# The order of the tensor engine's three pieces in an attention step: output products moved from behind the projection's part to directly behind the scores

## The chip, the cores and the metric

The kernel runs on one core of a Trainium2 chip. A core has a matrix engine (TensorE: PE in the profile, with PEld for its weight loads), three engines for elementwise work (VectorE: DVE, ScalarE: ACT, GpSimd: POOL), and a queue engine (SyncE: SP) that here only issues transfers. Each of them runs its own list of instructions in order, and they wait for each other through semaphores. The metric is the device time of the program in microseconds (us); before the change its median is 2392.17 us over 3 runs (2389.41 to 2393.09).

## The reference: what is computed

A transformer layer on an input x of 2 batches by 2048 tokens by 1024 channels, with 16 heads of width 64:

```python
x = x + layernorm(attention(layernorm(x)))
x = x + layernorm(ffn(layernorm(x)))
# attention
q, k, v = (x @ w.T + b for w, b in ...)           # heads of 64
scores = q @ k.T / 8, causal mask
out = softmax(scores) @ v;  out @ wo.T + bo
# ffn: 8 experts, a gate picks one per token, low-rank update of rank 8
```

The change concerns attention alone. The ffn follows in a later phase of the program.

## The kernel before, in words

**Pairs, rounds, steps.** The 32 (batch, head) problems are done as 16 pairs of heads (`p` = 0 to 15; pairs 8 to 15 are the second batch). In each pair the 16 query tiles of 128 rows are done two at a time, a long one and a short one, in 8 rounds. A round is cut into 2 or 3 steps of at most 8 key blocks of 128, a pair has 17 steps (`NSTEP`). A step whose `opens` is set starts a round, one whose `closes` is set ends it. In pairs 1 to 14 the closing steps are 1, 3, 5, 8, 10, 12, 14, 16; in pairs 0 and 15 they are 1, 3, 5, 7, 9, 11, 13, 16.

**What one step does on TensorE.** `body` of the tensor block runs three pieces per step `i`:

- `scores(i + 3)`: the score products of the step three further on (`LAG` = 3), for both heads, into two of three tiles `s_ps` (line 529). Every number is carried as a high and a low fp16 part, so each product is three matmuls. It waits until the exponential of an earlier task has freed its tile (`exp_done`).
- `project(...)`: a part of one projection unit of the next pair (lines 598 to 604). A unit is 512 tokens of q, k or v; it takes one step or is split over two (`UNIT_STEPS`). Its result lies in the one bank `u_ps`. The last matmul of a unit signals `unit_done`.
- `times_v(i, h)` for the two heads: transposed probabilities `pt` times v into `o_ps` (lines 552 to 554), 48 matmuls of 65 columns when the step has 8 blocks. It waits for the transposed tile (`pt_done`), and in an opening step also for `part_done` and `short_done`: the sums of the round before must have been read out of `o_ps`, of which there is one set.

**What follows each piece.** After the scores VectorE finds row maxima (`row_max`, lines 732, 737, 742), ScalarE takes exponentials and makes the high half (914, 921), GpSimd makes the low half (1072), and SyncE issues a transposing transfer for each head (419, `transpose_probs`), which waits until earlier output products have released their blocks of `pt` (`pv_done`). After a unit VectorE adds the bias and takes the result out of `u_ps` (`unit_full`, lines 711 for v and 716 for q and k). After a round VectorE reads `o_ps` (`output_read`, lines 760, 762, 766); line 766 signals `short_done`.

**VectorE's order in a step `i`.** `output_read` of the round that closed in step `i - 1` (only if `i` opens a round), `row_min`, `row_max(i + 3)`, `output_sum`, a weight's low half where one is due (698, 700), `unit_full` of the unit that ends in step `i`, and then, in pairs 0 to 6, pieces of the normalization of the second batch (`norm_stats` 661 and 668, `norm_apply` 676, `xn_low` 681; each of 16 tiles has one of each, every second or so step). This order isn't touched by the change.

**Which steps end a unit.** In pairs 1 to 5 and 8 to 13 ("mid"): 0, 1, 2, 4, 5, 7, 8, 10, 11, 13, 14, 16, of which v are 8, 10, 11, 13. In pair 0: 0, 1, 3, 5, 6, 7, 8, 10, 11, 13, 14, 16 (v: 8, 10, 11, 13). In pairs 6 and 7: 0, 1, 2, 4, 5, 6, 7, 9, 11, 12, 14, 16 (v: 1, 4, 9, 14). In pair 14: 1, 3, 5, 7, 9, 11, 13, 15 (k, k, k, q, q, v, v, v). In pair 15: 0, 1, 2, 4 (k, q, q, v), and from step 5 on that pair has no projection at all.

Of the kernel before, what the change touches and what calls it, by code (L numbers as in the profile page):

```python
# [188 lines left out]
def attend_phase(nc, x, w_pairs, mask_in, xn_scratch, o_scratch, arena, fin):  # L189
    with ExitStack() as ctx:  # L190
# [129 lines left out]
        def step_of(p, i, kind):  # L320

            if i + LAG < NSTEP:
                return p, i + LAG
            return None if kind == "last" else (p + 1, i + LAG - NSTEP)
# [13 lines left out]
        def units_before(p, needed):  # L338

            return N_UNIT * p + max(u for u, unit in enumerate(order_of(p)) if unit in needed) + 1  # L340
# [26 lines left out]
        def pt_of(n):  # L367
            return pt[:, 2 * PT_AT[n]:2 * (PT_AT[n] + TASK_BLOCKS[n]), :]
# [142 lines left out]
        def _(pe):  # L511
            def scores(p, i):
                n = NTASK * p + 2 * i
                for t, k0, nb, acc in steps_of(p)[i].parts:
                    pe.wait_ge(unit_lo_done, units_before(p, [("q", t // 4)] + [("k", c) for c in range((k0 + nb + 3) // 4)]))
                if n >= S_RING - 1:
                    pe.wait_ge(exp_done, n + 2 - S_RING)
                qk = nat[p % 2]
                q_hi, q_lo, k_hi, k_lo = range(4)

                at = 0
                for t, k0, nb, acc in steps_of(p)[i].parts:
                    rows, first, stop_at = slice(t * P, (t + 1) * P), at, at + nb * P
                    while at < stop_at:
                        end = min(stop_at, at // 512 * 512 + 512)
                        keys = slice(k0 * P + at - first, k0 * P + end - first)
                        for q, k in ((q_lo, k_hi), (q_hi, k_lo), (q_hi, k_hi)):
                            for h in range(2):
                                mm = nc.tensor.matmul(s_ps[(n + h) % S_RING][:, at:end], qk[HEADS[h], q, rows],  # L529
                                                      qk[HEADS[h], k, keys], start=(q == q_lo),  # L530
                                                      stop=(q == q_hi and k == k_hi))
                        at = end
                mm.then_inc(s_done, 2)

            def times_v(p, i, h):
                step, n = steps_of(p)[i], NTASK * p + 2 * i + h
                done = N_ROUND * p + step.round
                if h == 0:
                    for t, k0, nb, acc in step.parts:
                        pe.wait_ge(unit_lo_done, units_before(p, [("v", c) for c in range((k0 + nb + 3) // 4)]))  # L540
                pe.wait_ge(pt_done[n % T_RING], 16 * (n // T_RING + 1))
                if step.opens and h == 0 and done >= 1:
                    pe.wait_ge(part_done, done)
                    pe.wait_ge(short_done, done)
                blocks = [(k0 + k, acc) for t, k0, nb, acc in step.parts for k in range(nb)]
                for at, (k, acc) in enumerate(blocks):
                    hi, lo = pt_of(n)[:, at, :], pt_of(n)[:, step.blocks + at, :]
                    v_hi, v_lo = (v[p % 2][:, k, part, h, 0:HD + 1] for part in range(2))
                    dst = o_acc[:, acc, h, :]
                    first = step.opens and h == 0 and at == 0  # L550
                    last = step.closes and h == 1 and at == step.blocks - 1
                    nc.tensor.matmul(dst, lo, v_hi, start=first, stop=False)  # L552
                    nc.tensor.matmul(dst, hi, v_lo, start=False, stop=False)  # L553
                    mm = nc.tensor.matmul(dst, hi, v_hi, start=False, stop=last)  # L554
                mm.then_inc(pv_done, 1)
# [52 lines left out]
            def body(p, kind):  # L608
                for i in range(NSTEP):
                    step = step_of(p, i, kind)  # L610
                    if step:
                        scores(*step)
                    for u, part, count in UNIT_AT[kind][i:i + 1]:
                        atoms = ATOMS[order_of(units_of(p))[u][0]] // count
                        project(units_of(p), u, part * atoms, (part + 1) * atoms)
                    for h in range(2):
                        times_v(p, i, h)

            pe.wait_ge(consts_loaded, 32)
            for i in range(4):  # L620
# [17 lines left out]
            for i in range(LAG):  # L638
                scores(0, i)
                project(0, LAST_CHUNK + i, 0, ATOMS[order_of(0)[LAST_CHUNK + i][0]])  # L640
            pairs(body)

            pe.wait_ge(exp_done, NTASK * PAIRS)
# [1186 lines left out]
```

## Time and profile before

| | |
|---|---|
| median of 3 runs | 2392.17 us |
| profiled execution, its own time | 2388.15 us |
| its span, first to last instruction | 2386.0 us |
| TensorE busy | 2268.8 us (95%) |
| VectorE busy | 1693.1 us (71%) |
| ScalarE busy | 1745.6 us (73%) |
| GpSimd busy | 1654.4 us (69%) |
| granted TensorE clock, mean | 0.984 of full |
| attention steps | from about 72 to 1934 us of the span |

A matmul's end is modelled in this profile, so its listed duration is longer than the distance to the next one: the distance from start to start is what a matmul takes of the engine's time. "Idle before" in brackets at the end of a row is how long the engine stood still before the instruction, and behind the arrow is what ended it.

### The profile page before, as it was taken

What the parts mean: (1) busy time and instruction counts of PE and PEld (TensorE: products, weight loads), DVE (VectorE), ACT (ScalarE), POOL (GpSimd) and SP (SyncE); (2) the same over time, 40 slices, a digit from 0 to 9 for tenths busy, and PEclk for the clock granted to TensorE, in tenths of its full rate; (3) what the DMA queues carried; (4) which work ended last, traced back from release to release, by engine and by line L of the source; (5) the groups of instructions that cost most, each with busy time, mean ns of one, the idle gap of its engine ahead of it and who ended that gap; (6) DMA issues with size and microseconds to landing.
All of it is one profiled execution on the core that took longest, in us unless ns stands there. A gap on an engine that the chain in (4) does not pass through costs nothing. (4 is left out here: it accounts for less than half of the span.)

```text
span 2386.0 us, 70748 instructions
## 1 busy us (share of the span) xinstructions
PE 2268.8 (95%) x28698; PEld 1447.7 (61%) x28698; DVE 1693.1 (71%) x4148; ACT 1745.6 (73%) x2380; POOL 1654.4 (69%) x1291
## 2 busy tenths in 40 slices
PE   7999999999999998899999999999999579999996
PEld 5566767575757665557575757576766445545453
DVE  8577777777777765576666666666776947777777
ACT  6577787877777766577777777777887846666665
POOL 3588888888888876688888888888897822222221
PEclk9999999999999999999999999999999889999998
DMA  7799999999999999999999999999999976666662
GB/s 217 143 193 196 200 213 200 210 207 203 208 204 209 200 198 196 202 202 190 180 196 181 187 181 185 188 182 188 181 196 200 223 165 152 173 149 170 151 168 80
DMA packets 1372307, 445.33 MB, mean 187 GB/s; under 512 B 1316784, under 2 KB 1349952, under 8 KB 1371984
## 3 DMA queue, kind: packets, MB, share of 16 engines
q1 hardware_dynamic: 1371984, 440.81, 99.5%
q8 instruction: 228, 3.74, 0.6%
q14 instruction: 95, 0.78, 0.1%
HBM read 67.95 MB, written 41.94 MB: 46 GB/s over the span
## 5 line engine op out<-in xcount | busy, mean ns | idle before, releaser
L1072 POOL TENSOR_TENSOR hl<-probs,hl 128x1024 f16<-128x1024 f32 x544 | 1170.3, 2158 | 154.7 <-ACT hl L921 153.6
L914 ACT ACTIVATE probs<-s_ps,exp_bias 128x1024 f32<-128x1024 f32 (+7 forms) x768 | 633.1, 854 | 294.4 <-DVE exp_bias L742 293.9
L737 DVE TENSOR_REDUCE neg_max<-s_ps 128x1 f32<-128x1024 f32 (+7 forms) x768 | 676.8, 906 | 152.3 <-PE s_ps L529 149.3
L921 ACT ACTIVATE hl<-probs 128x1024 f16<-128x1024 f32 x544 | 575.0, 1057 | 78.0 <-DMA pt<-hl 61.9
L552 PE MATMUL o_ps<-v,pt 128*128 128x65 f16 x4352 | 430.8, 193 | 41.0 <-DMA pt<-hl 33.2
L552 PEld LDWEIGHTS o_ps<-v,pt 128*128 128x128 f16 x4352 | 400.5, 96 | 69.0 <-DMA pt<-hl 27.9
L529 PE MATMUL s_ps<-nat 64*128 64x512 f16 (+3 forms) x3840 | 408.4, 350 | 29.5 <-ACT probs L914 26.7
L553 PE MATMUL o_ps<-v,pt 128*128 128x65 f16 x4352 | 431.1, 194 | 0.0
L554 PE MATMUL o_ps<-v,pt 128*128 128x65 f16 x4352 | 429.8, 192 | 0.0
L553 PEld LDWEIGHTS o_ps<-v,pt 128*128 128x128 f16 x4352 | 399.7, 97 | 19.3
L554 PEld LDWEIGHTS o_ps<-v,pt 128*128 128x128 f16 x4352 | 400.2, 98 | 0.0
L602 PE MATMUL u_ps<-arena,w 128*128 128x512 f16 x1000 | 380.7, 381 | 5.1 <-DMA arena<-xn_scratch 3.0
L604 PE MATMUL u_ps<-arena,w 128*128 128x512 f16 x1000 | 379.0, 379 | 0.0
L603 PE MATMUL u_ps<-arena,w 128*128 128x512 f16 x1000 | 379.0, 379 | 0.0
L598 PE MATMUL u_ps<-w,arena 128*128 128x128 f16 x2016 | 347.1, 221 | 1.4 <-DVE arena L687 1.0
L599 PE MATMUL u_ps<-w,arena 128*128 128x128 f16 x2016 | 346.0, 220 | 0.0
L600 PE MATMUL u_ps<-w,arena 128*128 128x128 f16 x2016 | 345.9, 220 | 0.0
L529 PEld LDWEIGHTS s_ps<-nat 64*128 64x128 f16 x3840 | 162.6, 95 | 167.2 <-issue 38.2
L598 PEld LDWEIGHTS u_ps<-w,arena 128*128 128x128 f16 x2016 | 198.2, 98 | 42.7 <-issue 40.3
L1085 POOL TENSOR_TENSOR o_rows<-o_long,inv_long 128x128 f32<-128x128 f32 x128 | 76.4, 597 | 177.1 <-DVE inv_long L778 176.6
L599 PEld LDWEIGHTS u_ps<-w,arena 128*128 128x128 f16 x2016 | 198.5, 98 | 0.1
L600 PEld LDWEIGHTS u_ps<-w,arena 128*128 128x128 f16 x2016 | 198.5, 98 | 0.0
(190 smaller groups left out, 3633.9 us busy)
## 6 DMA issues: line engine op xcount, KB each, us to landing
w_raw<-in_w_pairs SPq DMA_DIRECT2D x46, 576.0 KB, 5.0
o_scratch<-o_hl SPq DMA_DIRECT2D x64, 256.0 KB, 3.1
out<-result SPq DMA_DIRECT2D x31, 512.0 KB, 3.2
x_in<-in_x SPq DMA_DIRECT2D x27, 512.0 KB, 4.9
pt<-hl SPq DMA_TRANSPOSE x544, 5.3
xn_scratch<-xn SPq DMA_DIRECT2D x16, 512.0 KB, 4.3
xn<-in_x SPq DMA_DIRECT2D x11, 512.0 KB, 3.9
x_in_c<-in_x SPq DMA_DIRECT2D x10, 512.0 KB, 4.0
```

Of the source, the lines that this page charges most:

```text
L529: mm = nc.tensor.matmul(s_ps[(n + h) % S_RING][:, at:end], qk[HEADS[h], q, rows], qk[HEADS[h], k, keys], start=(q == q_lo), stop=(q == q_h ...
L552: nc.tensor.matmul(dst, lo, v_hi, start=first, stop=False)
L553: nc.tensor.matmul(dst, hi, v_lo, start=False, stop=False)
L554: mm = nc.tensor.matmul(dst, hi, v_hi, start=False, stop=last)
L598: nc.tensor.matmul(dst, xt[:, 1, k, toks], hi[:, k, :], start=first, stop=False)
L599: nc.tensor.matmul(dst, xt[:, 0, k, toks], lo[:, k, :], start=False, stop=False)
L600: mm = nc.tensor.matmul(dst, xt[:, 0, k, toks], hi[:, k, :], start=False, stop=last)
L602: nc.tensor.matmul(bank, lo[:, k, :], xt[:, 0, k, toks], start=first, stop=False)
L737: nc.vector.tensor_reduce(neg_max[:, step.round, acc, h:h + 1], s_ps[(n + h) % S_RING][:, first:end], AX_X, ALU.max, negate=True).then_inc ...
L914: last = nc.scalar.activation(probs_of(n)[:, cols], s_ps[n % S_RING][:, cols], ACT.Exp, bias=exp_bias[:, step.round, acc, h:h + 1], scale= ...
L921: nc.scalar.activation(hl_of(n, 0), probs_of(n), ACT.Copy).then_inc(p_hi_done, 1)
L1072: nc.gpsimd.tensor_tensor(hl_of(n, 1), probs_of(n), hl_of(n, 0), ALU.subtract).then_inc(p_lo_done, 1)
```

## The change

The two output products of a step stood behind the projection's part; now they stand ahead of it, directly behind the scores. Nothing is added or removed, and no other engine's list changes: rows, waits and signals of VectorE, ScalarE, GpSimd and SyncE are the same.

```diff
                     if step:
                         scores(*step)
+                    for h in range(2):
+                        times_v(p, i, h)
                     for u, part, count in UNIT_AT[kind][i:i + 1]:
                         atoms = ATOMS[order_of(units_of(p))[u][0]] // count
                         project(units_of(p), u, part * atoms, (part + 1) * atoms)
-                    for h in range(2):
-                        times_v(p, i, h)
```

TensorE's list before, at the start of step 2 of pair 9 (an opening step): the scores of step 5 with their waits, then the projection's part (`u_ps`), which goes on for 24 rows.

```order
L529 MATMUL s_ps<-nat 128x512 [waits exp_done,unit_lo_done]
L529 MATMUL s_ps<-nat 128x512 x5
L529 MATMUL s_ps<-nat 128x128 x6
L529 MATMUL s_ps<-nat 128x384 x6
L602 MATMUL u_ps<-arena,w 128x512 [waits full_done,w_lo_done]
L603 MATMUL u_ps<-arena,w 128x512
```

The same place now: ahead of the scores stands the end of step 1's projection, and behind them the output products (`o_ps`) with their four waits.

```order
L603 MATMUL u_ps<-arena,w 128x512
L604 MATMUL u_ps<-arena,w 128x512
L529 MATMUL s_ps<-nat 128x512 [waits exp_done,unit_lo_done]
L529 MATMUL s_ps<-nat 128x512 x5
L529 MATMUL s_ps<-nat 128x128 x6
L529 MATMUL s_ps<-nat 128x384 x6
L552 MATMUL o_ps<-v,pt 128x65 [waits part_done,short_done,pt_done6,unit_lo_done]
L553 MATMUL o_ps<-v,pt 128x65
```

So the wait for `part_done` and `short_done` moved from behind a projection's part to directly behind the scores, and the projection's part of step 1 stands between the output products it waits the reading of and the scores.

VectorE's list, the same before and now, where a v unit ends in a closing step of pair 0 and a piece of the normalization stands in it: `unit_full`, the normalization piece, and behind them `output_read`.

```order
L711 SCALAR_TENSOR_TENSOR full<-u_ps,bv_row 128x512 [waits unit_lo_done,w_lo_done,unit_done]
L676 TENSOR_SCALAR x_in<-x_in,moments_a,rstd_a 128x1024 [waits rstd_done_a]
L760 TENSOR_TENSOR o_part<-o_ps,factor 128x260 [waits sum_done,factor_done,pv_done]
L762 RECIPROCAL inv_short<-o_ps 128x2
L766 TENSOR_TENSOR o_rows<-o_ps,inv_short 128x128 [waits o_lo_done,inv_short_done]
L751 TENSOR_REDUCE bias_min<-exp_bias 128x2 [waits factor_done,bias_done]
```

Nothing moved here: the reading of `o_ps` stands behind the wait for `unit_done`, as it did.

## Rows read from the trace of the kernel before

**Rows 1.** Busy time by stretch: width, PE, PEld, DVE, ACT, POOL, clock, DMA share, GB/s.

```profile
160.00:850.00 690.00, 685.62 (x9963) 462.15 (x9959) 521.93 (x1226) 543.33 (x703) 593.91 (x368) 1.00 1.15 204
850.00:1100.00 250.00, 225.79 (x3059) 145.26 (x3057) 156.96 (x384) 173.09 (x230) 184.20 (x111) 0.98 1.15 201
1100.00:1700.00 600.00, 600.00 (x8838) 407.59 (x8837) 406.69 (x1036) 465.82 (x612) 498.00 (x299) 1.00 1.09 185
1825.00:1940.00 115.00, 78.52 (x1141) 52.72 (x1138) 84.30 (x179) 84.45 (x112) 82.99 (x47) 0.84 1.10 218
```

**Rows 2.** Waits of the whole span: engine, line, waited for, us in total, times, longest.

```profile
PE o_ps L552 <- DMA pt<-hl: 33.2, 25, 4.0
...
PE o_ps L552 <- DVE o_rows L766: 7.4, 3, 3.5
```

**Rows 3.** Timeline, steps 1 and 2 of pair 9: start, length, engine, line.

```profile
1166.80 0.38 PE L604 MATMUL u_ps<-arena,w 128*128 128x512 f16 x1
...
1167.02 0.19 PE L552 MATMUL o_ps<-v,pt 128*128 128x65 f16 x1
...
1167.22 0.75 DVE L716 TENSOR_SCALAR full<-u_ps,bias_cols 128x512 f32<-128x512 f32 x1 [2.55 <-PE u_ps L604]
...
1168.56 1.48 PE L529 MATMUL s_ps<-nat 64*128 64x512 f16 x18
...
1168.67 0.43 DVE L760 TENSOR_TENSOR o_part<-o_ps,factor 128x260 f32<-128x260 f32 x1 [0.70 <-PE o_ps L554]
...
1169.21 0.29 DVE L766 TENSOR_TENSOR o_rows<-o_ps,inv_short 128x128 f32<-128x128 f32 x1
...
1169.97 0.39 PE L602 MATMUL u_ps<-arena,w 128*128 128x512 f16 x1
```

**Rows 4.** Timeline of PE, pair 15, a step without projection, V to S to V.

```profile
1853.18 0.19 PE L554 MATMUL o_ps<-v,pt 128*128 128x65 f16 x1
1853.31 1.47 PE L529 MATMUL s_ps<-nat 64*128 64x512 f16 x12
1854.71 0.20 PE L552 MATMUL o_ps<-v,pt 128*128 128x65 f16 x1
```

**Rows 5.** Timeline of PE, from a projection's part to scores, at 87 us.

```profile
87.36 0.38 PE L604 MATMUL u_ps<-arena,w 128*128 128x512 f16 x1
87.67 1.47 PE L529 MATMUL s_ps<-nat 64*128 64x512 f16 x12
```

**Rows 6.** Timeline, pair 1, closing step 10, where a v unit ends.

```profile
285.27 0.22 PE L600 MATMUL u_ps<-w,arena 128*128 128x128 f16 x1
...
285.53 0.69 DVE L711 SCALAR_TENSOR_TENSOR full<-u_ps,bv_row 128x512 f32<-128x512 f32 x1
286.14 2.04 DVE L681 SCALAR_TENSOR_TENSOR xn<-x_in,xn 128x1024 f16<-128x1024 f32 x1
288.10 0.42 DVE L760 TENSOR_TENSOR o_part<-o_ps,factor 128x260 f32<-128x260 f32 x1
```

**Rows 7.** Timeline, pair 15: an opening step's output products directly behind scores.

```profile
1888.35 1.19 PE L529 MATMUL s_ps<-nat 64*128 64x384 f16 x10
...
1891.12 0.29 DVE L766 TENSOR_TENSOR o_rows<-o_ps,inv_short 128x128 f32<-128x128 f32 x1
...
1891.56 0.19 PE L552 MATMUL o_ps<-v,pt 128*128 128x65 f16 x1 [2.02 <-DVE o_rows L766]
```

**Rows 8.** VectorE's groups by line, 160 to 850 us: count, busy us, mean ns.

```profile
L681 DVE SCALAR_TENSOR_TENSOR xn<-x_in,xn 128x1024 f16<-128x1024 f32 x14 | 28.1, 2005 | 0.0
L676 DVE TENSOR_SCALAR x_in<-x_in,moments_a,rstd_a 128x1024 f32<-128x1024 f32 x15 | 21.9, 1460 | 0.0
...
L661 DVE BATCH_NORM_STATS2 stats_a<-x_in 128x6 f32<-128x512 f32 x30 | 19.2, 681 | 0.9 <-DMA x_in<-in_x 0.9
```

**Rows 9.** SyncE's own waits, whole span: us in total, times, longest.

```profile
SPq L419 <- PE o_ps L554: 590.9, 301, 5.8
```

**Rows 10.** All idle time of TensorE ahead of line 552, whole span: us, times.

```profile
  DMA pt<-hl: 61.1, 45
```

## The prediction

> **What bounds the kernel now.** I read the busy time by stretches first, then the waits, then single steps on the timeline. In the middle of the attention (1100 to 1700 us) TensorE is busy 600.00 of 600 us at full clock, and from 160 to 850 us 685.62 of 690; VectorE is busy 522 of those 690 [rows 1]. So between about 160 and 850 and between 1100 and 1700 us every microsecond that TensorE stands still is added to the time, and there is almost no idle time there to win. Idle time lies only where SyncE's transposes run late: 24 us of the 250 between 850 and 1100 us, and 36 us of the last pair's stretch, where from step 5 on no projection is left to move [rows 1]. The waits say the same: ahead of the output products TensorE stood still 61.1 us in 45 places for a transposed tile [rows 10], and for VectorE's reading of `o_ps` only 3 times, 7.4 us [rows 2]. Those three lie in the last pair, where output products already stand directly behind scores [rows 7]. That is the order which the change makes the rule.
>
> **The change: matmuls and their borders.** The count of matmuls stays. Three borders per step change: before V to S, S to P, P to V; after P to S, S to V, V to P (P projection, S scores, V output products). A block of scores, from its first matmul to the next piece's first, takes 1.41 us before P (1168.56 to 1169.97) [rows 3] and 1.40 before V [rows 4]. Entering scores costs a little beyond the last matmul's own time: from V 0.13 us against a V matmul's 0.03 [rows 4], from P 0.31 against 0.22 [rows 5, 3], so about 0.1 from both. P to V is 0.22, the P matmul's own time [rows 3]. V to P is not shown; I take nothing extra, as for P to V, with 0 below and 0.1 above (the cost of entering scores), times the 259 steps that have both: 0 to +26 us, taken 0.
> The Trainium skill ("TensorE: Matmul & The Clock Gate", "Step-by-step: what each phase is for") says weights may be loaded ahead of running matmuls when the row groups do not conflict. [...]
>
> **The change: the wait for the sums.** An opening step's V waits until VectorE has read the last round's sums out of `o_ps`. Before, a whole projection part lay between S and V, 2.4 to 5.2 us long, and hid the reading. Now V follows S. VectorE's list is fixed: in the closing step it waits for the end of the unit (`unit_full`), does a normalization piece if one is due, and only then reads `o_ps`. The sums are ready one projection part earlier than before, but VectorE cannot take them while it stands at `unit_done`. Let t be the start of the part's last matmul, in a closing step that ends a q or k unit:
> VectorE starts `unit_full` at t + 0.42 and needs 0.75 (1166.80, 1167.22) [rows 3]; the next instruction starts 0.08 before the end (286.14 against 285.53 + 0.69) [rows 6], so at t + 1.09; the three instructions of the reading take 0.83 (1168.67 to 1169.50) [rows 3]: t + 1.92; V starts 0.15 after them (1891.41 to 1891.56) [rows 7]: t + 2.07. TensorE alone would be there at t + 0.31 + 1.40 = t + 1.71 [rows 5, 4]. It stands still for 0.36 us.
> For a v unit: start t + 0.26, 0.69 long [rows 6], so reading from t + 0.87 to t + 1.70, V at t + 1.85. The matmuls are a quarter as wide, so the border to S is 0.31 less three quarters of 0.22, 0.15, and TensorE is there at t + 1.55. It stands still for 0.30 us.
> How often: a mid pair has six such steps (closing and ending a unit: 1, 5, 14, 16 for q or k, 8 and 10 for v); eleven mid pairs give 44 and 22. Pair 0 gives 5 and 2, pairs 6 and 7 three and two each, pair 14 three, pair 15 one: 59 and 28. 59 x 0.36 = 21.2 and 28 x 0.30 = 8.4, together 29.6 us. The bounds of one such wait are 0 (the reading hidden) and 2.0 (rows 7's wait, behind other VectorE work).
>
> **The change: normalization pieces ahead of the reading.** In pairs 0 to 6 the pieces (3 for each of 16 tiles) fall on steps 7 x tile + 2, + 4, + 6. Eighteen of the 48 fall on a closing step that ends a unit, six of each kind. There they stand between `unit_full` and the reading, and nothing hides them any more: before, V (1.5 us) and S did, and in step 10 of pair 1 the reading began at 288.10 behind a 2.04 us piece without TensorE waiting [rows 6]. Their lengths are 2.01 (681), 1.46 (676) and two of 0.68 (661, the small aggregate not counted) [rows 8], less the 0.08 of overlap: 6 x (1.93 + 1.38 + 1.28) = 27.5 us. Six more fall on closing steps that end no unit; VectorE is not held there and has part of the time: 0 to 1.9 each, I take 4 us for all.
>
> **The change: transposed tiles.** V now comes one part (2.4 to 5.2 us) sooner after its scores. In the two full stretches TensorE has no wait for tiles worth naming, and SyncE itself stands 590.9 us for V to release blocks [rows 9]; that gate opens as much earlier as V runs, so the tiles keep their lead. Where the queue is behind (850 to 1100 us, and pair 14 with its short steps) the earlier V meets a late tile; the queue's own work sets the pace there, so what is lost is about one part once: 0 to 10, taken 3. Against it, of the waits summed above some ten lie in those stretches, where TensorE would have stood anyway: minus 3.
>
> Sum: 29.6 + 27.5 + 4 + 3 - 3 = 61 us on the profiled 2388.15 us, 2449 us. The median of the runs lies 4 us above that execution, so I forecast 2392.17 + 61 = 2453 us.
> The Trainium skill ("Perfetto Trace Analysis", "Optimizing Tensor Performance") says that independent groups of matmuls should rotate through different banks of PSUM, so that one is evacuated while the next runs. Here the rounds share one `o_ps`, and what hid the evacuation was the projection in another bank. The rule speaks against this order; the three waits of the last pair agree [rows 2, 7].
>
> **Rivals.**
> *Waits for the sums only, the pieces cost nothing.* VectorE's pieces would have to be hidden by S, as one was by V and S together [rows 6]. S alone is 1.4 us and the reading is already late without a piece, which speaks against it. 2392 + 30 = 2422 us. 8 in 100.
> *VectorE's lateness runs on.* The row maxima of the next scores start behind the reading, so exponentials and the next scores get late, or the pieces' and the idle time's share takes the clock down, as in the stretch with 24 of 250 us idle, where the clock was 0.98 [rows 1]; or V to P costs a border. For it: VectorE is 76% busy from 160 to 850 us. Against: the next scores come a V and a P later, 4 us. With 0.1 us more at each of 259 steps, or as much from the other two, 2453 + 26 = 2479 us. 15 in 100.
> *Tiles late all along.* If the tiles did not move with V, they would be late wherever their lead is shorter than a part; with one part of 2.4 us lost in each of 8 rounds of pairs 6, 7 and 14, it is 24 x 2.4 = 58 us more, 2511 us. The 590.9 us of the gate speak against it. 4 in 100.
> *Faster.* Blocks of `pt` are released a part earlier, so transposes start earlier where SyncE waited for them [rows 9]; of the 24 us of idle time between 850 and 1100 us up to 20 vanish, and the reading is hidden because it ends before S does: 2372 us. The point from which it decides is 1.71 us behind t: the reading has to be over by then, and I find 1.92. 4 in 100, and as much for no change, the same mechanism at a third of its size against a few waits.
>
> **How the numbers follow.** The forecast has 65 in 100; its own range is 2438 to 2468 us (half to one and a half of the 27.5 + 4, rounded). The range of 8 in 10 takes in most of the first two rivals: 2420 to 2482 us. About 0.2% (5 us) is what a measurement of this kernel can tell from no change. Faster by more: 0.04; within: 0.04; slower: 0.92.
>
> **What would show it.** In the new profile: waits of TensorE's line 552 for VectorE's 766 rise from 3 to about 90 or more and some 60 us in sum, nearly all in opening steps; the shortest are near 0.36 and 0.30 us, those of pairs 0 to 6 with a piece between 1.5 and 2.5 us. VectorE no longer waits for line 554 ahead of 760. TensorE busy between 1100 and 1700 us falls to about 590 of 600, and a mid pair of the second batch grows by 2.0 us, one of the first by 5 to 9. Wrong would be: a rise mostly from waits for `pt`, from ScalarE's 914 ahead of the scores, or longer borders without a wait.

## The result and the profile after

The change makes the kernel slower: 2464.23 us median (2463.05 to 2464.71, 4 runs) against 2390.79 us for the kernel before on the same chip, a ratio of 1.0305 with a 95% interval of 1.0291 to 1.0318. The forecast was 2453 us in a range of 2420 to 2482. The profiled execution has a span of 2461.7 us, 75.7 us more than before.

First the busy time of the kernel after by stretches, with the columns of [rows 1]:

```profile
160.00:850.00 690.00, 641.91 (x9097) 424.09 (x9094) 484.98 (x1136) 500.14 (x649) 541.04 (x340) 0.98 1.03 187
850.00:1100.00 250.00, 223.77 (x3140) 146.04 (x3137) 151.00 (x370) 166.22 (x219) 178.60 (x108) 0.97 1.12 194
1100.00:1700.00 600.00, 592.15 (x8439) 383.04 (x8436) 395.52 (x1019) 458.68 (x599) 491.28 (x292) 1.00 1.05 183
1825.00:1940.00 115.00, 105.72 (x1607) 70.60 (x1603) 77.74 (x205) 90.45 (x122) 93.02 (x56) 0.98 1.12 199
```

Against [rows 1], TensorE's idle time between 160 and 850 us has grown from 4 to 48 us and the granted clock there has fallen from 1.00 to 0.98; between 1100 and 1700 us it stands idle 8 us where it stood idle not at all, at full clock. (The last row cannot be set beside its counterpart: the last pair begins later now.) The second thing to read is who waited for whom, whole span, TensorE's rows:

```profile
PE o_ps L552 <- DVE o_rows L766: 76.5, 92, 3.7
PE o_ps L552 <- DMA pt<-hl: 31.3, 22, 3.3
PE s_ps L529 <- ACT probs L914: 17.2, 13, 3.6
```

The wait for VectorE's reading of `o_ps`, 7.4 us in 3 places before, is 76.5 us in 92 [rows 2]. The wait for transposed tiles has hardly moved (33.2 us in 25 places before). On SyncE's side the gate did open earlier, as its own waits show: its wait for output products fell from 590.9 us [rows 9] to 404.9 and its wait for GpSimd's halves rose from 49.2 to 207.6, without a gain in time.

```profile
SPq L419 <- PE o_ps L554: 404.9, 245, 5.9
SPq L418 <- POOL hl L1072: 207.6, 148, 4.8
```

Now a single short wait, VectorE and TensorE around an opening step of the second batch. It answers to [rows 3]:

```profile
1217.93 1.48 PE L529 MATMUL s_ps<-nat 64*128 64x512 f16 x18
1219.67 0.19 PE L552 MATMUL o_ps<-v,pt 128*128 128x65 f16 x1 [0.27 <-DVE o_rows L766]
...
1218.04 0.75 DVE L716 TENSOR_SCALAR full<-u_ps,bias_cols 128x512 f32<-128x512 f32 x1 [1.41 <-PE u_ps L604]
1218.71 0.42 DVE L760 TENSOR_TENSOR o_part<-o_ps,factor 128x260 f32<-128x260 f32 x1
...
1219.24 0.29 DVE L766 TENSOR_TENSOR o_rows<-o_ps,inv_short 128x128 f32<-128x128 f32 x1
```

VectorE stands idle for 1.41 us at the unit's end (line 716), although the sums that it could read were ready long before; then it takes the unit out, reads the sums (1218.71 to 1219.53), and V starts 0.14 us later. From the first score matmul to V it is 1.74 us; where nothing holds V it is 1.41, as here one step on:

```profile
1226.39 1.47 PE L529 MATMUL s_ps<-nat 64*128 64x512 f16 x12
1227.80 0.20 PE L552 MATMUL o_ps<-v,pt 128*128 128x65 f16 x1
```

The lost time is 0.33 us, and the row's own 0.27 is smaller by the modelled end of the last score matmul. A long wait, step 11 of pair 1, which answers to [rows 6]:

```profile
303.08 1.48 PE L529 MATMUL s_ps<-nat 64*128 64x256 f16 x18
307.53 0.21 PE L552 MATMUL o_ps<-v,pt 128*128 128x65 f16 x1 [2.97 <-DVE o_rows L766]
307.56 0.24 PE L553 MATMUL o_ps<-v,pt 128*128 128x65 f16 x1
307.61 0.25 PE L554 MATMUL o_ps<-v,pt 128*128 128x65 f16 x1
...
303.19 0.69 DVE L711 SCALAR_TENSOR_TENSOR full<-u_ps,bv_row 128x512 f32<-128x512 f32 x1 [1.50 <-PE u_ps L600]
303.80 2.85 DVE L681 SCALAR_TENSOR_TENSOR xn<-x_in,xn 128x1024 f16<-128x1024 f32 x1
306.57 0.41 DVE L760 TENSOR_TENSOR o_part<-o_ps,factor 128x260 f32<-128x260 f32 x1
```

The same piece that cost nothing before now keeps TensorE for 3.04 us (4.45 from the first score matmul to V, less 1.41). And behind it the V matmuls start 0.05 us apart, not 0.03: the clock has fallen to its lower level, 1.2 GHz. The same shows around a wait of 2.92 us that ends at 610.88 us: from 608 to 616 us the mean granted clock is 0.79, against 1.00 in the kernel before.

```profile
608.00:616.00 8.00, 5.12 (x59) 3.75 (x60) 6.85 (x19) 3.35 (x7) 1.92 (x3) 0.79 0.59 111
```

**Where the 75.7 us are.** Span less busy time of TensorE was 117.2 us and is 172.4: 55.2 us more idle. The waits for line 766 alone grew by 69.1 us (7.4 to 76.5), so TensorE's other idle time shrank by 13.9; 9.5 of these are waits for ScalarE ahead of the scores (26.7 to 17.2 us), 1.9 are waits for tiles. Busy time rose from 2268.8 to 2289.3 with the same matmuls: 20.5 us, which are the lower clock and, at each new wait, up to 0.07 us of modelled end. From the mean clocks, 0.984 and 0.976, the time at the lower level is 2 x 0.016 x 2386 = 76 us before and 2 x 0.024 x 2461.7 = 118 us after. These are one execution each: the other executions of the kernel before have mean clocks of 0.977 to 0.983 at the same time, and a thousandth of the clock is 5 us here, so the 42 us are rough. The stretch from 160 to 850 us shows the fall more clearly, 1.00 against 0.98.

By pair, from the scores of its first step to those of the next pair's, pairs 0 to 5 grew by 2.3, 19.2, 6.4, 5.4, 10.8 and 13.0 us, pairs 6 and 7 by 2.8 and 5.3, pair 8 shrank by 0.4, pairs 9 to 13 grew by 1.8 each, pair 14 by 2.5. In pair 1, the largest, TensorE stands idle 13 us more and works 6 us longer for the same matmuls; its waits for line 766 are 14.5 us in 7 places, and the clock falls three times in it.

### The profile page after: what moved, and what is told of

The parts are those of the page before. It is cut to its first block and busy times, and to the rows that moved or that the text cites. A ratio compares the mean times of both kernels' runs of the same rounds, so it can differ in the third digit from the quotient of the medians.

```text
span 2461.7 us, 70748 instructions
## 1 busy us (share of the span) xinstructions
PE 2289.3 (93%) x28698; PEld 1435.1 (58%) x28698; DVE 1687.4 (69%) x4148; ACT 1747.4 (71%) x2380; POOL 1651.2 (67%) x1291
## 5 line engine op out<-in xcount | busy, mean ns | idle before, releaser
L552 PE MATMUL o_ps<-v,pt 128*128 128x65 f16 x4352 | 442.0, 195 | 110.6 <-DVE o_rows L766 76.5
L552 PEld LDWEIGHTS o_ps<-v,pt 128*128 128x128 f16 x4352 | 402.7, 97 | 222.0 <-issue 180.9
L553 PE MATMUL o_ps<-v,pt 128*128 128x65 f16 x4352 | 441.0, 196 | 0.0
L554 PE MATMUL o_ps<-v,pt 128*128 128x65 f16 x4352 | 440.2, 194 | 0.0
L529 PE MATMUL s_ps<-nat 64*128 64x512 f16 (+3 forms) x3840 | 403.6, 348 | 20.1 <-ACT probs L914 17.2
L554 PEld LDWEIGHTS o_ps<-v,pt 128*128 128x128 f16 x4352 | 405.9, 99 | 0.0
L553 PEld LDWEIGHTS o_ps<-v,pt 128*128 128x128 f16 x4352 | 405.3, 98 | 0.0
L716 DVE TENSOR_SCALAR full<-u_ps,bias_cols 128x512 f32<-128x512 f32 x125 | 93.8, 750 | 307.6 <-PE u_ps L604 300.1
L598 PEld LDWEIGHTS u_ps<-w,arena 128*128 128x128 f16 x2016 | 199.3, 99 | 2.7 <-DVE arena L687 1.4
L599 PEld LDWEIGHTS u_ps<-w,arena 128*128 128x128 f16 x2016 | 199.2, 99 | 0.1
```

The costliest lines, as they stand in the source:

```text
L598: nc.tensor.matmul(dst, xt[:, 1, k, toks], hi[:, k, :], start=first, stop=False)
L599: nc.tensor.matmul(dst, xt[:, 0, k, toks], lo[:, k, :], start=False, stop=False)
```

## The experiments

The theory: V's place decides when TensorE asks for the sums to be read, VectorE's list decides when it reads them, and the second is tied to the end of the unit. The rivals: the earlier V meets late tiles, the borders between pieces cost, or VectorE is simply overloaded. Times are ratios to the kernel before, run on the same chip beside each.

### e1_read_first: the reading ahead of the wait for the unit

```diff
                     if evacuate:
-                        output_read(*done)
...
                     if evacuate:
                         output_sum(*done)
+                    if steps_of(p)[i].closes:
+                        output_read(p, r)
...
                 if kind == "last":
-                    output_read(p, N_ROUND - 1)
```

> The changed kernel, with VectorE's reading of o_ps (760, 762, 766) moved in its own list: in a closing step it stands ahead of unit_full and of the normalization piece instead of behind them. Theory (the reading is late because it is queued behind the wait for the unit's end): all waits of line 552 for line 766 in pairs 0 to 14 go, with them the half-clock stretches between 160 and 850 us, and the time comes back to the kernel before, 2380 to 2395 us. Rival (the earlier V itself, late tiles or the borders are what costs): no more than the first half-microseconds go, and it stays above 2440 us.

Measured: 2406.33 us, ratio 1.0075 (1.0063 to 1.0087). No wait for line 766 is left in pairs 0 to 14. Pairs 9 to 13 are as long as before to a tenth of a microsecond; TensorE is busy all the time there:

```profile
160.00:850.00 690.00, 674.52 (x9769) 443.70 (x9764) 516.33 (x1205) 531.87 (x689) 585.31 (x363) 1.00 1.11 200
1100.00:1700.00 600.00, 600.00 (x8764) 396.33 (x8763) 405.40 (x1035) 467.75 (x615) 502.52 (x298) 1.00 1.06 184
```

So 56 of the 73 us (73.4 less the 17.1 that are left) hang on one place in VectorE's list, and V's new place by itself costs nothing in pairs 9 to 13 of the second batch: neither borders nor tiles. But the forecast of 2380 to 2395 failed by 11 us: something else costs about 17 us in the first batch and in the change between batches. Its waits between 160 and 850 us say what it looks like (before: 3.8 us for ScalarE, none for tiles):

```profile
PE s_ps L529 <- ACT probs L913: 9.2, 12, 1.3
PE o_ps L552 <- DMA pt<-hl: 6.2, 7, 1.9
```

### e2_opening_only and e3_other_steps_only: the change in half of the steps

```diff
-                    for h in range(2):
-                        times_v(p, i, h)
+                    if steps_of(p)[i].opens:         # e3: if not ...opens
+                        for h in range(2):
+                            times_v(p, i, h)
                     for u, part, count in UNIT_AT[kind][i:i + 1]:
...
+                    if not (steps_of(p)[i].opens):   # e3: if ...opens
+                        for h in range(2):
+                            times_v(p, i, h)
```

> V stands ahead of the projection's part only in steps that open a round; in all others it stays behind it. Theory: the waits for the sums arise in opening steps alone, but here the V before (of the closing step) stands at the end of its step as in the kernel before, so VectorE reads it behind the end of V, not behind the end of the unit: reading ends about 1.2 us after the last V matmul starts, scores take 0.12 + 1.40 us, so it is just hidden, unless a piece is queued: 2395 to 2430 us. Rival (the place of the opening V alone decides): the same as the full change, near 2464 us.

> V stands ahead of the projection's part only in steps that do not open a round; in opening steps a projection's part still lies between the scores and V. Theory: the reading is hidden again by that part and the time is that of the kernel before, 2385 to 2396 us. Rival (earlier V costs by late tiles): between the two, 2405 us or more.

Measured: e2 2405.97 us, ratio 1.0070 (1.0053 to 1.0087), as expected; the wait for line 766 is 14.5 us in 20 places, 11.6 of it between 160 and 850 us, where the pieces are. Neither half alone makes the waits of the whole: it takes the closing step's V ahead of the unit's last matmul and the opening step's V directly behind the scores. e3 gave 2416.35 us, ratio 1.0116 (1.0100 to 1.0131), where I had expected no change: a miss. Its waits for line 766 are 6.0 us in 4 places, no more than before (7.4 us in 3), so the theory held for those; the second batch's pairs 9 to 13 are again exactly as long as before. What grew most is the wait for tiles: over the span 61.8 us in 43 places against 33.2 in 25, and between 850 and 1100 us, shown here, against 13.6 in 11.

```profile
PE o_ps L552 <- DMA pt<-hl: 27.4, 20, 3.6
```

Between 160 and 850 us there are 8.0 us of it, against none, and the wait for ScalarE ahead of the scores is 14.6 us in 15 places, against 3.8 in 5 (over the whole span that one fell, from 26.7 to 23.3). So the time lies in the range of the rival that was put on record, late tiles, and the rows bear it out. Why e3 meets more late tiles than the full change, which has 31.3 us of them, no run shows.

### e4_second_batch_only: pairs 8 to 15

```diff
+                    if p >= HALF_PAIRS:
+                        for h in range(2):
+                            times_v(p, i, h)
...
+                    if not (p >= HALF_PAIRS):
+                        for h in range(2):
+                            times_v(p, i, h)
```

> V stands ahead of the projection's part in pairs 8 to 15 only; pairs 0 to 7 are as before. Theory: in the second batch there are no normalization pieces, so six short waits (0.17 to 0.34 us) and their drains make 1.8 us for each mid pair, 11 us in all with pair 14: about 2400 us. Rival (half of the slowing per pair, whatever the batch): 2425 us.

Measured: 2401.28 us against 2387.73, ratio 1.0058 (1.0041 to 1.0075), 13.5 us; pairs 8 to 13 grew by 1.8 to 1.9 each and TensorE's idle time between 1100 and 1700 us is the 8 us of the full change. The slowing of a second-batch pair is the short waits and nothing else, and five sixths of the whole lie ahead of it: pairs 0 to 7 grew by 65 of the 76 us that the pairs sum to.

### e5_pieces_behind: the pieces out of the way

```diff
                     if opens:
                         row_min(p, r)
+                    if evacuate:
+                        pieces(*((p, i - 1) if i else (p - 1, NSTEP - 1)))
                     step = step_of(p, i, kind)
                     if step:
                         row_max(*step)
...
-                    for tile in norm_tiles(p, i, 0): ...
+                    if not steps_of(p)[i].closes:
+                        pieces(p, i)          # the three loops over norm_tiles
```

> The changed kernel, with the normalization pieces of closing steps taken out from between unit_full and the reading of o_ps and put directly behind the reading in VectorE's list. Theory: the 24 long waits (1.3 to 3.3 us, about 45 us together) shrink to the 0.2 to 0.35 us of the others and the half-clock stretches of the first batch go with them (about 34 us at half clock, some 17 us of time): 2400 to 2415 us. Rival (clock falls for another reason, or the pieces' time comes back as late maxima and scores): above 2430 us.

Measured: 2420.02 us, ratio 1.0128 (1.0115 to 1.0142); 43 us of the 73 are gone with the pieces' place (73.4 less 30.8). The time is 5 us above the forecast of 2400 to 2415 and below the rival's 2430. Between 160 and 850 us the wait for line 766 went from 47.0 us in 35 places to 8.3 in 32, and the clock is back at 1.00:

```profile
160.00:850.00 690.00, 673.59 (x9750) 443.76 (x9749) 509.17 (x1201) 532.59 (x689) 580.00 (x362) 1.00 1.11 200
```

The waits for the sums there are 38.7 us shorter (47.0 less 8.3), while those for ScalarE ahead of the scores rose from 1.1 to 6.2 us and those for tiles from nothing to 1.6. That leaves 32 us of the 43. The other 11 are the clock's share and what lies outside this stretch; no run tells the two apart.

### e6_longer_queue and e7_longer_queue_old_order: an artificial piece

```diff
+                    if steps_of(p)[i].closes and HALF_PAIRS <= p < PAIRS - 2 and units_ending(kind, i):
+                        for half in range(2):
+                            nc.vector.tensor_scalar(xn[:, half * D:(half + 1) * D], x_in[:], 1.0, None, ALU.mult)
```

The same lines stand in VectorE's list behind the normalization pieces, once in the changed kernel (e6), once in the kernel before (e7).

> The changed kernel with two copies of 1024 columns (about 0.8 us each, into a tile that nothing reads then) added to VectorE's list in pairs 8 to 13, in the 36 closing steps that end a unit, between unit_full and the reading of o_ps: an artificial normalization piece where there is none. Theory: each of the 36 waits grows by the whole 1.5 us, 54 us or more over the changed kernel, about 2518 us; and if the long waits are what takes the clock down in the first batch, half-clock stretches appear between 1100 and 1700 us too, and the time rises beyond 2525 us. Rival (VectorE's added work hides): under 2480 us.

> The kernel before (V behind the projection's part) with the same two copies in the same 36 places of VectorE's list. Theory: the projection's part between the scores and the next V hides them, and the time stays within 4 us of the kernel before, about 2391 us. Rival (VectorE's 57 us of added work costs by itself): 2410 us or more.

Measured: e6 2625.0 us, ratio 1.0992 (1.0972 to 1.1012); e7 2417.67 us, ratio 1.0122 (1.0104 to 1.0139). Both missed their numbers, because the added copies are longer than I took them for: 1.69 us each on average in e6 and 1.74 in e7, not 0.8 (means of 50 and 62 of the 72 copies, between 1100 and 1700 us). Two pairs of these copies in e6, and GpSimd's instructions beside them:

```profile
1172.36 2.69 DVE L837 TENSOR_SCALAR xn<-x_in 128x1024 f16<-128x1024 f32 x2
...
1187.91 5.06 DVE L837 TENSOR_SCALAR xn<-x_in 128x1024 f16<-128x1024 f32 x2
```

```profile
1171.77 2.13 POOL L1075 TENSOR_TENSOR hl<-probs,hl 128x1024 f16<-128x1024 f32 x1
...
1185.66 6.75 POOL L1075 TENSOR_TENSOR hl<-probs,hl 128x1024 f16<-128x1024 f32 x3
```

The first pair began when GpSimd had 1.54 us of its instruction left (to 1173.90); its first copy took until 1174.45, 2.09 us, and its second, with GpSimd idle, 0.68. The second pair lay almost wholly beside GpSimd's three instructions and took 5.06 us. The Trainium skill ("SBUF — State Buffer", "SBUF: two separate sides") says that VectorE and GpSimd share one pair of ports as an exclusive lock, for a VectorE instruction in a two-port mode or with two inputs in SBUF, and whoever comes second blocks for the whole instruction. The trace agrees with the blocking: the first copy took the 1.54 us that GpSimd had left and 0.55 more. In which mode the copy runs, no row says. With the measured length the two experiments speak clearly. The artificial pieces add 36 x 2 x 1.7 = 122 us of work to VectorE. With V in its new place they cost 161 us over the changed kernel, all of them and more. With V in the old place they cost 30 us, a quarter. That is not nothing: e7 lies in the range of its rival (2410 us or more), so VectorE's added work costs something by itself, and the rows show it as a wait for ScalarE ahead of the scores, 19.1 us in 15 places between 1100 and 1700 us. And the stretch that was at full clock in every other kernel is not any more:

```profile
1100.00:1700.00 600.00, 513.17 (x6802) 338.33 (x6801) 399.33 (x872) 373.49 (x489) 405.54 (x239) 0.93 0.81 148
```

```profile
1100.00:1700.00 600.00, 579.59 (x8376) 389.52 (x8374) 488.68 (x1044) 444.39 (x581) 502.75 (x285) 1.00 1.02 178
```

In e6 (first row) TensorE waits 86.8 us in 26 places for line 766 there, 3.3 us each, and the mean granted clock is 0.93, so 2 x 0.07 x 600 = 84 us of the 600 at 1.2 GHz; in e7 (second row) no wait exceeds 1.7 us, and it is 1.00. The clock follows the waits, not the batch. Whether it is their length or their share of the time that counts is not separated here: e6 has both, with TensorE idle 87 of 600 us.

### e8_read_first_old_order: e1's list for VectorE, TensorE as before

The edit is that of e1_read_first, made in the kernel before.

> The kernel before with the reading of o_ps ahead of unit_full in VectorE's list, as in e1_read_first, but TensorE's order as before. With V at the end of the step the unit's result is then taken out of u_ps about 1.6 us later. Theory: nothing waits for it that soon (the next part comes behind scores), and TensorE does not change: 2387 to 2396 us. Rival (the 17 us that e1_read_first stays above the kernel before come from VectorE's new order, not from the earlier V): 2400 us or more here.

Measured: 2431.26 us, ratio 1.0180 (1.0165 to 1.0195), a miss by more than 35 us and in the range of the rival (2400 us or more). With V at the end of the step VectorE now waits for V before it takes the unit out of `u_ps`, and the next projection part finds `u_ps` still full. Between 1100 and 1700 us:

```profile
PE u_ps L602 <- DVE full L716: 7.4, 27, 0.3
PE u_ps L598 <- DVE full L711: 2.0, 10, 0.2
```

I had counted 1.4 us of scores as cover for a reading and an evacuation of 1.6 together. That is the mirror image of the change: whichever of V and the projection comes last on TensorE, VectorE must serve first the one that came first. It also means that e1_read_first's rest does not show VectorE's new list as good or bad by itself; the list fits one order of TensorE.

### e9, e10, e11: the pieces ahead of the wait for the unit

```diff
-                    for u in units_ending(kind, i):
-                        unit_full(units_of(p), u)
                     for tile in norm_tiles(p, i, 0): ...
+                    for u in units_ending(kind, i):
+                        unit_full(units_of(p), u)
```

In e9 on top of e1_read_first, in e10 in the changed kernel, in e11 in the kernel before.

> As e1_read_first, and the normalization pieces too ahead of unit_full, where VectorE otherwise stands idle for the unit's end. Theory for the 17 us that e1_read_first kept: scores now come directly behind the projection's part (before, a V of 1.5 us lay between), so unit_full and a piece push the next row maxima behind the end of the scores and the exponentials late; with the pieces first the waits of line 529 for ScalarE in the first batch (9.2 us) and of line 552 for tiles (6.2 us) shrink to under 8 us together, and the time to 2392 to 2402 us. Rival (those waits come from the transfers' queue): no change against e1_read_first, 2404 to 2408 us.

> The changed kernel with the normalization pieces ahead of unit_full; the reading of o_ps stays behind unit_full. Theory: the pieces lie in VectorE's idle time before the unit's end where the part is long, so the long waits mostly shrink to the short ones: 2410 to 2425 us, no worse than e5_pieces_behind (2420 us). Rival (a long queue of VectorE, wherever the piece stands, makes the long waits): above 2440 us.

> The kernel before with the normalization pieces ahead of unit_full. TensorE has almost no wait in the first batch to lose, so theory: the same time, 2386 to 2394 us. Rival (unit_full behind a piece holds up the next projection part or the next maxima): 2397 us or more.

Measured: e9 2400.52 us, ratio 1.0040 (1.0025 to 1.0055); e10 2412.07 us, ratio 1.0097 (1.0080 to 1.0114); e11 2391.11 us, ratio 1.0006 (0.9997 to 1.0015). All three times as the theory said, but one wait in e9 not. The pieces fill VectorE's idle time at the unit's end. Of e9's waits between 160 and 850 us, that for ScalarE fell from 9.2 us to 3.1, the level of the kernel before; that for tiles did not fall (9.8 us in 6 places against 6.2 in 7):

```profile
PE o_ps L552 <- DMA pt<-hl: 9.8, 6, 3.4
PE s_ps L529 <- ACT probs L913: 3.1, 3, 1.3
```

So the rest of e1_read_first has at least two parts. One was late row maxima: V no longer lies between a unit's last matmul and the next scores, so what VectorE does at a unit's end delays the maxima. The other shows as tiles that V asks for too early, in the first batch (9.8 us against none before) and between 850 and 1100 us (16.6 us in 13 places against 13.6 in 11); no experiment takes this part away. With both lists suited to the new order the kernel is still some 10 us slower than before (0.4%, interval 0.25 to 0.55%). No version here beats the kernel before; e11 ties with it.

## Why the prediction was right, point by point

- **What bounds the kernel.** Right: in the second batch each wait reappears in the time (pairs 9 to 13 grew by 1.8 us; the six waits of such a pair sum to 1.47, and the other 0.3 is what their rows leave out by the modelled end of the scores, 0.06 us in each as in the worked case above), and it vanishes with them (e1_read_first).
- **The borders.** Right. Of the 259 borders from V to a projection part 247 take 0.03 us, V's own matmul, and 12 take 0.05 or 0.06, as V's matmuls themselves do at the lower clock; entering scores costs what it did from the projection, 0.31 us. The reach up to 26 us was not used.
- **The short waits.** Forecast 0.36 and 0.30 us at 59 and 28 places. The worked case came out as 1219.67 - 1217.62 = 2.05 us from the start of the part's last matmul (0.31 ahead of the scores' first at 1217.93) to V, against 2.07. The 67 places without a piece sum to 18.8 us by their rows, 0.28 on average, and to about 22 with the modelled ends, where I had 23.5 for 69: slightly too high.
- **The pieces.** This is the term that was too small. Eighteen places were right to the last one. Their waits sum to 40.0 us, of which 6 are the short wait's share; 34 stand against 27.5 forecast. They lie between 1.1 and 3.3 us where the forecast had 1.5 to 2.5. The pieces are longer in the places where they now stand (between 160 and 850 us line 681 takes 2.34 us on average, 13 of them, against 2.01, line 676 1.58 against 1.46) [rows 8], and some of these waits are in part at the lower clock. The six places without a unit's end: 4.9 us in 3 places, 4 forecast. The growth of a pair of the first batch, forecast at 5 to 9 us, held for pairs 2 and 3 (6.4 and 5.4) and failed for 1, 4 and 5 (19.2, 10.8 and 13.0), where most of the waits behind pieces and the lower clock are.
- **The clock.** Not in the sum but only in a rival, which I gave 15 in 100. It belonged in the sum: twice the fall of the mean clock gives 42 us more at the lower level, and TensorE's busy time rose by 20.5 us, about 14 of it by the clock. It alone has the size of what is missing, 61 forecast and 73 measured, but see the next point. The idle share (48 of 690 us) was not much above what I had worked out; what I did not do was to look at the single gap. Between 160 and 850 us the clock fell within 1.5 us of the end of eight waits, at 183, 238, 292, 308, 461, 611, 662 and 765 us, which are 2.2 to 3.3 us long. At three others of that size (2.56 us at 199, 2.37 at 256, 2.72 at 397) the granted clock stayed at 1.00, and at those under 2 us it did too.
- **The sum.** It came nearer than its parts. The waits for line 766 grew by 69 us where the forecast had 61: 6.5 more from the pieces, 5.4 in the last pair, which the forecast left as it was, and 1 where no unit ends, less 5 of the short ones by their rows. The lower clock and the modelled ends add 20.5, and 14 us of other waits went away, where the forecast had allowed 3. That these last two cancel in part was luck.
- **Tiles.** The forecast was 3 lost and 3 given back. In the changed kernel right: 33.2 us before, 31.3 after. But e1, e3 and e9 showed that this was partly because the waits for the sums hid the lateness: once they are gone, 6 to 10 us of tile waits come out in the first batch. The lead that I said they keep is shorter there than I took it to be.
- **The rivals.** Shown wrong: tiles late all along (58 us), pieces at no cost, faster. The rival "VectorE's lateness runs on" was half right: its clock part came, its late-maxima part is hidden in the changed kernel (1.1 us between 160 and 850) and appears in e1 (9.2 us).

What stays open: how e9's remaining 10 us split between late tiles in the first batch and the change between batches, and whether the lower clock comes from the length of the waits or from their share. Neither was tried.

## What to carry to other kernels

A wait costs what is queued ahead of the instruction that ends it. When a piece of the busiest engine is moved, look at the lists of the engines that serve it: the one that serves two results in a fixed order must meet them in the order in which they are made, or it stands idle at one while the other is waited for (e1, e8). And cost waits of 2 us and more twice on TensorE: once as idle time, and once, as it showed here at eight of eleven of them between 160 and 850 us, as work at the lower clock.

## What the hardware did that I had not expected

- Waits of 2.2 to 3.3 us each were enough for the lower clock: it was 0.98 over 690 us with 35 waits for the sums (47.0 us, the longest 3.3), and in e6 0.93 over 600 us with 26 of them (86.8 us, the longest 5.2).
- A VectorE instruction on 1024 columns that takes 0.68 us alone took 2.5 beside GpSimd (two in 5.06 us), so that a list's length depends on where it falls, not only on what is in it.
- Entering the score matmuls (64 rows) costs about 0.1 us from either neighbour (0.13 us against 0.03 from V, 0.31 against 0.22 from the projection), while the border between V and the projection costs nothing in either direction (0.03 us from V, 0.22 into V).
